# Windowed attention with 64x32 row tiles on TensorE, one head per half of the array, keys and values without zero blocks, and the feed-forward hidden layer in one PSUM bank

## The chip, the core and the metric

The kernel runs on one NeuronCore of a Trainium2 chip. A core has five engines that run side by side: TensorE (PE in the profile; its weight loads are shown as PEld), VectorE (DVE), ScalarE (ACT), GpSimd (POOL) and SyncE (SP), which here only issues DMAs. They are kept in step by semaphores. The metric is device time in microseconds for one execution; the kernel before takes 2605.0 us as the median of three runs (2604.25 to 2606.4).

## The reference

Eight sequences of 256 tokens and 128 channels pass through four stages, each wrapped in a layer norm before and after and a residual. Stage 1 is a linear attention, stage 2 is a stack of six layers of windowed attention plus gated feed-forward, stage 3 is a causal attention with a position bias, stage 4 is a mixture of eight experts. The change is in stage 2, whose layer is:

```
x = attn_layer(shift_tokens(x)) + x
x = ffn_layer(shift_tokens(x)) + x

attn_layer: q, k, v = split(x @ Wqkv)          # 16 heads of 64
            q, k = rotary(l2norm(q)), rotary(l2norm(k))
            window of 32 queries sees its own 32 keys and the 32 before
            sim = 8 * q @ k.T, masked; attn = softmax(sim); out = attn @ v
            return concat(out) @ Wo
ffn_layer:  a, gate = split(layernorm(x) @ W1 + b1)   # 341 wide each
            return (a * gelu(gate)) @ W2 + b2
```

All of it is in fp32.

## The kernel before

Stage 2 treats a (layer, sequence) pair as one item, so there are 6 x 8 = 48 items. The program is a software pipeline of steps t, each of eight slots s = 0 to 7, written out by hand in the same order on each engine (`step` at the end of each engine's part). In step t, item t is projected and rotated, item i = t - 1 goes through attention, and item f = t - 2 through the output projection and the feed-forward. The order of the code is the order of the work; every engine takes its instructions in that order and waits on semaphores.

The pieces, with the lines by which the profile names them:

- `projection` (PE L527): 512 columns of q or k for 128 tokens, one per slot, into bank 0 or 1. `squares` (ACT L900) and `parts` (DVE L1211) read it; `norms` (DVE L1218) follows at each odd slot, and POOL rotates and normalises (L1519 to L1527). `turn` (PE L538) transposes the rotated piece four slots later; `take_turned` (ACT L922 for queries, L925 and L926 for keys) copies it to `qT` or `kT`.
- `kT` holds for each pair of heads two blocks of 64 rows times keys: head 0 in rows 0 to 63 of the first, head 1 in rows 64 to 127 of the second, and zeros elsewhere. So one matmul with 128 rows and 32 columns of weights (the queries of one window, both heads) streams 2 x 64 columns and gives both heads' scores. `scores` (PE L563) does this for 4 pairs and 4 windows: 16 matmuls that write four 32-partition strips of bank 3. The bank has been seeded with the mask by `seed` (DVE L1235).
- `shift_scores` (DVE L1223, L1227) subtracts the row maximum, `exps` (ACT L933) takes the exponential, `turn_probs` (PE L572) transposes, `take_probs` (ACT L938) copies.
- `values` (PE L548) makes v; `take_values` (ACT L912) copies its two 64-row halves to `vp`, where each head has 64 columns and a one, with zeros in the other head's half of the rows; SP copies every second window's rows by DMA (`spread_values`). `weigh` (PE L584) is again 16 matmuls per group, 128 rows by 32 columns of weights, streaming 130 columns. `divide_out` (DVE L1241, L1245) divides by the sum, `turn_out` (PE L595, into bank 4) and `take_out` (ACT L945) give the transposed output.
- `project_out` (PE L604), a layer norm (L412, L418, POOL L1531, L425, DVE L1101 to L1110, L1258), `hidden` (PE L618) for three blocks c = 0, 1, 2 of the feed-forward, `gelu` (ACT L951), `gate` (DVE L1264), `contract` (PE L626) and two residual adds (DVE L1252, L1270). The three blocks of `hidden` use banks 2, 4 and 2, so block 1 shares a bank with `turn_out`.

Exp and Gelu need different ACT function tables, so ACT loads a table twice per item, before the first `gelu` and before the `exps` after the last.

Each fp32 matmul appears as two records in the trace (and its weight load as two), a transpose as one.

Of the kernel before, what the change touches and what calls it, by code (L numbers as in the profile page):

```python
# [33 lines left out]
VB = 2 * (DH + 1)  # L34
# [36 lines left out]
HD_BANK = (2, 4, 2)  # L71
# [9 lines left out]
def build(nc, a, out):  # L81
    ctx = ExitStack()
    with ctx:
# [6 lines left out]
        bank = [ctx.enter_context(nc.psum_tensor(f"bank{i}", [P, 512], F32)) for i in range(5)]  # L90
# [48 lines left out]
        kT = sb("kT", [P, PAIRS, 2, KW])  # L139
# [15 lines left out]
        kTf = kT[:, :, :, :].rearrange("p a b t -> p (a b t)")  # L155
# [21 lines left out]
        bias = kTf[:, 0:H * S].rearrange("p (h t) -> p h t", h=H)  # L177
# [15 lines left out]
        mw2 = vflat[:, NE * EF:2 * NE * EF].rearrange("p (e c n) -> p e c n", e=NE, c=4)  # L193
# [77 lines left out]
        def _(sp):  # L271
# [73 lines left out]
            def layer(l, first, last):  # L345
                for n in range(B):
                    t = l * B + n
                    sp.wait_ge(v_done, 8 * t + 2)
# [8 lines left out]
                    sp.wait_ge(v_done, 8 * t + 4)  # L357
# [12 lines left out]
                    sp.wait_ge(v_done, 8 * t + 6)  # L370
# [8 lines left out]
                    sp.wait_ge(v_done, 8 * t + 8)  # L379
# [16 lines left out]
            sp.dma_start(bias, bass.AP(relu_dram.ap().tensor, 0, [[1, P], [384, H], [1, S]])).then_inc(rel_in, 16)  # L396
# [11 lines left out]
        def _(pe):  # L408
# [132 lines left out]
            def values(i, w, odd):  # L541
# [4 lines left out]
                wait(pe, v_done, 8 * i + 2 * w)  # L546
# [6 lines left out]
            def scores(i, k):  # L553
# [21 lines left out]
            def weigh(i, k):  # L575
# [31 lines left out]
            def hidden(i, c):  # L607
# [4 lines left out]
                if c == 1:  # L612
                    wait(pe, ot_done, 4 * i + 4 + min(3, 4 * (ITEMS - 1 - i)))
                if c == 2:
                    pe.wait_ge(h_done, 3 * i + 1)
                n = P if c < 2 else FFR
                for half in range(2):
                    mm = nc.tensor.matmul(bank[HD_BANK[c]][0:n, half * S:half * S + S], w1[:, half * FF + c * P:half * FF + c * P + n],  # L618
# [53 lines left out]
            nc.tensor.matmul(bank[3][:, :], ident_bf, maskv[:, 0, :], start=True, stop=True).then_inc(seeded, 1)  # L672
# [176 lines left out]
        def _(act):  # L849
# [52 lines left out]
            def take_values(i, j):  # L902
# [803 lines left out]
```

## Time and profile before

| | value |
|---|---|
| median of 3 runs | 2605.0 us (2604.25 to 2606.4) |
| the profiled execution's own time | 2607.13 us |
| its span | 2605.3 us |
| stage 2 in full flow, as cut here | 250 to 1950 us |
| one step in full flow | 37.21 us |
| mean granted TensorE clock | 0.967, 1.00 in full flow |

Times in the profile are microseconds from the start of the span. The busy time of an engine is the union of its instructions; matmuls overlap in the array, so a record of 275 ns may advance the engine by much less. In full flow the steps repeat to within a hundredth of a microsecond, so the rows of one step stand for all. The step shown starts with the projection of slot 1 at 1052.68 and ends with that of the next step at 1089.89; its slots 2 to 7 start their projections at 1056.82, 1060.58, 1064.28, 1068.54, 1072.94 and 1078.20, and slot 0 of the next step at 1082.82.

### The profile page before, as it was taken

Reading aid. Unit: us, or ns where it says so; the run is one execution under the profiler, and the core shown is the slowest. Engines: PE = TensorE matmul, PEld = TensorE weight load, DVE = VectorE, ACT = ScalarE, POOL = GpSimd, SP = SyncE. Lnnn points to the kernel's source line nnn. Section 1 sums busy time; section 2 is a strip of 40 time slices with the busy share of each in tenths; the row PEclk is TensorE's granted clock in tenths of the full one; section 3 lists DMA queues with packets and bytes.
Section 4 is the critical chain, followed back from the end, with each engine's and each line's share of the span. In section 5 each row is a group of like instructions: output and inputs, shape, how many; then the busy total and the mean of one; then the engine's idle time right before and its main releaser. Section 6 shows DMA issues by size and latency. Waiting matters only on the chain.

```text
span 2605.3 us, 57541 instructions
## 1 busy us (share of the span) xinstructions
PE 2383.1 (91%) x22655; PEld 1632.9 (63%) x22655; DVE 1763.3 (68%) x2708; ACT 1625.6 (62%) x3162; POOL 1605.3 (62%) x931
## 2 busy tenths in 40 slices
PE   5769999999999999999999999999997888889998
PEld 3436666666666666666666666666665666656665
DVE  2348777777777777777777777777774888852332
ACT  1127777777777777777777777777773666643332
POOL 1039878887888788878887888788872222301111
PEclk8879999999999999999999999999997999989999
DMA  4002223222232222322233222322223000000000
GB/s 107 0 21 59 53 55 75 69 63 55 59 79 69 55 59 62 78 63 59 53 78 71 59 54 54 87 66 54 54 56 102 1 1 1 1 1 5 5 2 8
DMA packets 77196, 127.11 MB, mean 49 GB/s; under 512 B 24948, under 2 KB 48770, under 8 KB 76930
## 3 DMA queue, kind: packets, MB, share of 16 engines
q1 hardware_dynamic: 76930, 123.42, 20.3%
q8 instruction: 184, 3.01, 0.5%
q14 instruction: 82, 0.67, 0.1%
HBM read 26.56 MB, written 1.07 MB: 11 GB/s over the span
## 4 chain that ended last, share of the span: by engine, by line
PE 45%; DVE 26%; issue 13%; ACT 12%; POOL 4%; DMA 0%; SPq 0%; ACTq 0%; POOLq 0%; DVEq 0%
DVE qk L1211 7%; PE bank L604 7%; PE bank L527 5%; PE bank L563 5%; PE bank L813 4%; PE obank L584 4%; DVE n L1218 4%; PE bank L618 3%; ACT qk L900 3%; DVE bank L1235 3%; PE obank L823 2%; PE bank L823 2%; DVE sh L1227 2%; DVE mx L1223 2%; DVE mx L1365 2%
## 5 line engine op out<-in xcount | busy, mean ns | idle before, releaser
L1211 DVE TENSOR_TENSOR qk<-bank,tab 128x1024 f32<-128x1024 f32 x384 | 468.7, 1221 | 308.4 <-ACT qk L900 308.4
L1519 POOL TENSOR_TENSOR qk<-qk 128x1024 f32<-128x1024 f32 x192 | 454.6, 2368 | 284.0 <-DVE qk L1211 284.0
L1523 POOL TENSOR_TENSOR rn<-n2m,cst 128x16 f32<-128x16 f32 x192 | 562.6, 2930 | 16.0
L527 PE MATMUL bank<-wqk,xs 128*128 128x512 f32 x768 | 404.4, 609 | 46.0 <-ACT kT L926 43.0
L1527 POOL TENSOR_TENSOR qk<-qk,rn 128x1024 f32<-128x1024 f32 x192 | 365.2, 1902 | 28.2 <-POOL rn L1523 0.9
L900 ACT ACTIVATE qk<-bank 128x512 f32<-128x512 f32 x384 | 227.1, 591 | 213.8 <-PE bank L527 208.4
L538 PEld LDWEIGHTS bank<-cst,qk 128*128 128x128 f32 x1536 | 192.3, 141 | 210.5 <-issue 186.4
L1531 POOL TENSOR_TENSOR lnr<-lnv,cst 128x2 f32<-128x2 f32 (+1 forms) x88 | 66.3, 753 | 382.4 <-DVE lnv L1105 382.4
L538 PE MATMUL bank<-cst,qk 128*128 128x128 f32 x1536 | 231.7, 274 | 7.5 <-POOL qk L1527 7.5
L1218 DVE TENSOR_REDUCE n<-qk 128x16 f32<-128x1024 f32 x192 | 232.1, 1209 | 0.0
L912 ACT COPY vp<-lnbank 64x512 f32<-64x512 f32 x384 | 225.0, 586 | 9.4
L933 ACT ACTIVATE px<-sh 128x512 f32<-128x512 f32 x192 | 121.0, 630 | 153.9 <-DVE sh L1227 153.3
L563 PE MATMUL bank<-kT,qT 128*32 128x128 f32 x6144 | 208.0, 275 | 7.6 <-DVE bank L1235 1.3
L584 PE MATMUL obank<-vp,pT 128*32 128x130 f32 x6144 | 209.2, 274 | 0.0
L548 PE MATMUL lnbank<-wv,xs 128*64 128x512 f32 x768 | 208.0, 620 | 0.0
L563 PEld LDWEIGHTS bank<-kT,qT 128*32 128x32 f32 x6144 | 159.0, 109 | 50.8 <-issue 32.7
L527 PEld LDWEIGHTS bank<-wqk,xs 128*128 128x128 f32 x768 | 134.5, 191 | 78.1 <-ACT kT L926 54.6
L604 PE MATMUL bank<-aoT,wo 128*128 128x256 f32 x768 | 178.6, 385 | 0.7 <-DVE Z L1270 0.7
L595 PEld LDWEIGHTS bank<-cst,ao 128*128 128x128 f32 x768 | 80.3, 140 | 155.4 <-issue 153.4
L584 PEld LDWEIGHTS obank<-vp,pT 128*32 128x32 f32 x6144 | 177.3, 110 | 0.3 <-issue 0.3
L618 PE MATMUL bank<-lnt,w 128*128 128x256 f32 (+1 forms) x576 | 157.3, 397 | 2.7 <-DVE lnt L1258 1.7
L604 PEld LDWEIGHTS bank<-aoT,wo 128*128 128x128 f32 x768 | 142.0, 190 | 27.9 <-issue 10.5
(195 smaller groups left out, 4387.8 us busy)
## 6 DMA issues: line engine op xcount, KB each, us to landing
vp<-vp SPq DMA_DIRECT2D x672, 130.0 KB, 2.4
wqk<-in_L_ffn_Wqkv SPq DMA_DIRECT2D x24, 256.0 KB, 3.1
wv<-in_L_ffn_Wqkv SPq DMA_DIRECT2D x6, 512.0 KB, 3.6
wo<-in_L_ffn_Wo SPq DMA_DIRECT2D x6, 512.0 KB, 4.2
xs<-Z SPq DMA_DIRECT2D x48, 64.0 KB, 2.0
xs<-Z SPq DMA_DIRECT2D x48, 63.8 KB, 2.0
kT<-rel_by_distance SPq DMA_DIRECT2D x1, 2048.0 KB, 8.1
vp<-in_L_ffn_w SPq DMA_DIRECT2D x1, 2048.0 KB, 13.2
```

The lines of the kernel that those rows point to most:

```text
L527: nc.tensor.matmul(bank[s % 2][:, :], xs[:, odd, WIN + r * P:WIN + r * P + P], wqk[:, lo:lo + 512], start=True, stop=True).then_inc(p_full, 1)
L538: mm = nc.tensor.transpose(bank[(s + 1) % 2][:, q * P:q * P + P], rot[:, c, q * P:q * P + P], ident)
L563: mm = nc.tensor.matmul(s[WIN * w:WIN * w + WIN, q * P:q * P + P], qT[:, 4 * g + q, lo:lo + WIN], keys if w % 2 else keys[:, :, ::-1, :], ...
L584: mm = nc.tensor.matmul(obank[WIN * w:WIN * w + WIN, q // 2, (q % 2) * VB:(q % 2) * VB + VB], pT[:, k % 2, q * P + w * WIN:q * P + w * WIN ...
L604: mm = nc.tensor.matmul(bank[2][:, 0:S], wo[:, c, :], aoT[:, c, :], start=(c == 0), stop=(c == PAIRS - 1))
L618: mm = nc.tensor.matmul(bank[HD_BANK[c]][0:n, half * S:half * S + S], w1[:, half * FF + c * P:half * FF + c * P + n], lnt[:, S:2 * S], sta ...
L900: nc.scalar.activation(qk[:, square_of(s), :], bank[s % 2][:, :], ACT.Square).then_inc(sq_done, 1)
L1211: tt(qk[:, both, :].rearrange("p o (h d) -> p o h d", d=DH), heads(bank[c % 2][:, :]).unsqueeze(1).broadcast_to([P, 2, PAIRS, DH]), table. ...
L1218: red(n2[:, m % 2, :], qk[:, lo:lo + 2, :].rearrange("p a (h d) -> p (a h) d", d=DH), AX, ALU.add).then_inc(n2_raw, 1)
L1519: tt(direct, direct, swapped, ALU.add).then_inc(sum_done, 1)
L1523: tt(rn[:, m % 2, :], n2m[:, :], const("mhalf"), ALU.pow).then_inc(rn_done, 1)
L1527: tt(whole, whole, rn[:, m % 2, :].unsqueeze(2).broadcast_to([P, H, DH]), ALU.mult).then_inc(rot_done, 1)
```

## The change

`kT` has one block per pair, with head 0 in rows 0 to 63 and head 1 in rows 64 to 127, and no zeros; `vp` has 65 columns per pair instead of 130. A matmul of `scores` and of `weigh` now uses 64 rows and 32 columns, for one head. There are 32 per group instead of 16, each streaming 64 (65) columns instead of 128 (130). Head 0's results go to one PSUM bank and head 1's to the next: banks 3 and 4 (`sbank`) for scores, the two of `obank` for the weighing. Bank 4 is therefore no longer free for `turn_out`, which moves to the second bank of `obank`, nor for block 1 of `hidden`, which moves to bank 2. So each block of `hidden` now waits until `gate` has read the block before. The mask seed goes to half of two banks. ACT copies a group of keys, and a block of values, with one instruction instead of two. On ACT, `gelu` of block 0 moves from the start of slot 5 to behind `take_turned`; on DVE `gate` of block 0 moves behind `norms`. The scratch of stage 3 (the bias) and stage 4 (`w2` of the experts) that lived in the halved tensors has other places; `relu_dram` is read by two DMAs.

```diff
-VB = 2 * (DH + 1)
+VB = DH + 1
...
-        bank = [ctx.enter_context(nc.psum_tensor(f"bank{i}", [P, 512], F32)) for i in range(5)]
+        bank = [ctx.enter_context(nc.psum_tensor(f"bank{i}", [P, 512], F32)) for i in range(3)]
+        sbank = ctx.enter_context(nc.psum_tensor("sbank", [P, 2, 512], F32))
+        bank += [sbank[:, 0, :], sbank[:, 1, :]]
...
-        kT = sb("kT", [P, PAIRS, 2, KW])
+        kT = sb("kT", [P, PAIRS, KW])
...
-                s = bank[3]
                 for q in range(4):
                     for w in range(4):
                         lo = r * P + w * WIN
-                        keys = kT[:, 4 * g + q, :, lo:lo + 2 * WIN].rearrange("p o (s j) -> p o s j", s=2)
-                        mm = nc.tensor.matmul(s[WIN * w:WIN * w + WIN, q * P:q * P + P], qT[:, 4 * g + q, lo:lo + WIN],
-                                              keys if w % 2 else keys[:, :, ::-1, :], start=False, stop=True,
-                                              skip_group_check=True)
+                        for o in range(2):
+                            own = slice(64 * o, 64 * o + 64)
+                            keys = kT[own, 4 * g + q, lo:lo + 2 * WIN].rearrange("p (s j) -> p s j", s=2)
+                            mm = nc.tensor.matmul(sbank[WIN * w:WIN * w + WIN, o, q * DH:q * DH + DH],
+                                                  qT[own, 4 * g + q, lo:lo + WIN],
+                                                  keys if w % 2 else keys[:, ::-1, :], start=False, stop=True,
+                                                  skip_group_check=True)
...
                 wait(pe, ao_done, 4 * i + k)
+                wait(pe, ot_done, 4 * i + k)
                 for q in range(4):
                     for w in range(4):
-                        mm = nc.tensor.matmul(obank[WIN * w:WIN * w + WIN, q // 2, (q % 2) * VB:(q % 2) * VB + VB],
-                                              pT[:, k % 2, q * P + w * WIN:q * P + w * WIN + WIN],
-                                              vp[:, 4 * r + w, 4 * g + q, :], start=True, stop=True)
+                        for o in range(2):
+                            own = slice(64 * o, 64 * o + 64)
+                            mm = nc.tensor.matmul(obank[WIN * w:WIN * w + WIN, o, q * VB:q * VB + VB],
+                                                  pT[own, k % 2, q * P + w * WIN:q * P + w * WIN + WIN],
+                                                  vp[own, 4 * r + w, 4 * g + q, :], start=True, stop=True)
...
             def turn_out(i, k):
                 pe.wait_ge(ao_done, 4 * i + k + 1)
-                wait(pe, ot_done, 4 * i + k)
-                if k == 3 and i >= 1:
-                    pe.wait_ge(h_done, 3 * i - 1)
                 for q in range(4):
-                    mm = nc.tensor.transpose(bank[4][:, q * P:q * P + P], ao[:, k % 2, q * P:q * P + P], ident)
+                    mm = nc.tensor.transpose(obank[:, 1, q * P:q * P + P], ao[:, k % 2, q * P:q * P + P], ident)
...
-                if c == 1:
-                    wait(pe, ot_done, 4 * i + 4 + min(3, 4 * (ITEMS - 1 - i)))
-                if c == 2:
-                    pe.wait_ge(h_done, 3 * i + 1)
+                else:
+                    pe.wait_ge(h_done, 3 * i + c)
...
-                for o in (1, 0):
-                    lo = 64 * o
-                    src = vbank[lo:lo + 64, :].rearrange("p (a d) -> p a d", d=DH)
-                    cols = slice(o * (DH + 1), o * (DH + 1) + DH)
-                    nc.scalar.copy(vp[lo:lo + 64, 2 * j + 1, :, cols], src).then_inc(v_done, 1)
+                nc.scalar.copy(vp[:, 2 * j + 1, :, 0:DH], vbank[:, :].rearrange("p (a d) -> p a d", d=DH)).then_inc(v_done, 1)
...
-                    nc.scalar.copy(kT[0:64, pairs, 0, lo:lo + P], src[0:64])
-                    last = nc.scalar.copy(kT[64:P, pairs, 1, lo:lo + P], src[64:P])
+                    last = nc.scalar.copy(kT[:, pairs, lo:lo + P], src)
...
-                    if s in (5, 7) and p2:
-                        gelu(f, s - 5)
+                    if s == 7 and p2:
+                        gelu(f, 2)
...
-                    if s == 6 and p2:
-                        gelu(f, 1)
+                    if s in (5, 6) and p2:
+                        gelu(f, s - 5)
```

The first place is ACT in slots 5 and 6 of a step. Before, it read (L951 is `gelu`, L933 `exps`, L900 `squares`, L925 and L926 the keys' copies, L945 `take_out`, L938 `take_probs`):

```order
L933 ACTIVATE px<-sh 128x512 [waits pt_full,sh_done]
L951 ACT_TABLE_LOAD
L951 ACTIVATE ge<-bank,b1g 128x256 [waits hd_full]
L900 ACTIVATE qk<-bank 128x512 [waits n2_raw,p_full]
L925 COPY kT<-bank 64x4x128 [waits sc_full,t_full]
L926 COPY kT<-bank 64x4x128
L945 COPY aoT<-bank 128x4x128 [waits ot_full]
L938 COPY pT<-obank 128x512 [waits o_full,pt_full]
L900 ACTIVATE qk<-bank 128x512 [waits n2_raw,p_full]
```

Now it reads (L952 is `gelu`, L906 `squares`, L927 the keys' copy):

```order
L934 ACTIVATE px<-sh 128x512 [waits pt_full,sh_done]
L906 ACTIVATE qk<-bank 128x512 [waits n2_raw,p_full]
L927 COPY kT<-bank 128x4x128 [waits sc_full,t_full]
L952 ACT_TABLE_LOAD
L952 ACTIVATE ge<-bank,b1g 128x256 [waits hd_full]
L946 COPY aoT<-obank 128x4x128 [waits ot_full]
L939 COPY pT<-obank 128x512 [waits o_full,pt_full]
L906 ACTIVATE qk<-bank 128x512 [waits n2_raw,p_full]
```

The table load and the first `gelu` have moved behind the squares of slot 5 and the keys' copy, and that copy is one instruction.

The second place is PE from slot 6 to the projection of slot 7. Before, it read (L618 is `hidden`, blocks 1 and 2, L563 `scores`, L584 `weigh`):

```order
L538 MATMUL bank<-cst,qk 128x128 x3
L618 MATMUL bank<-lnt,w 128x256 [waits ot_done]
L618 MATMUL bank<-lnt,w 128x256
L563 MATMUL bank<-kT,qT 32x128 [waits seeded,t_done]
L563 MATMUL bank<-kT,qT 32x128 x15
L584 MATMUL obank<-vp,pT 32x130 [waits ao_done,pt_done]
L584 MATMUL obank<-vp,pT 32x130 x15
L618 MATMUL bank<-lnt,w 85x256 [waits h_done]
L618 MATMUL bank<-lnt,w 85x256
L527 MATMUL bank<-wqk,xs 128x512 [waits t_done]
```

Now it reads (L623 is `hidden`, L569 `scores`, L594 `weigh`):

```order
L543 MATMUL bank<-cst,qk 128x128 x3
L623 MATMUL bank<-lnt,w 128x256 [waits h_done]
L623 MATMUL bank<-lnt,w 128x256
L569 MATMUL sbank<-kT,qT 32x64 [waits seeded,t_done]
L569 MATMUL sbank<-kT,qT 32x64 x31
L594 MATMUL obank<-vp,pT 32x65 [waits ot_done,ao_done,pt_done]
L594 MATMUL obank<-vp,pT 32x65 x31
L623 MATMUL bank<-lnt,w 85x256 [waits h_done]
L623 MATMUL bank<-lnt,w 85x256
L532 MATMUL bank<-wqk,xs 128x512 [waits t_done]
```

The sequence is the same; there are twice as many small matmuls of half the width, and the first `hidden` row waits for `gate` of block 0 instead of for a copy out of bank 4.

## Rows read from the trace of the kernel before

**Rows 1.** The page: span, and busy time of each engine with its share.
```profile
span 2605.3 us, 57541 instructions
PE 2383.1 (91%) x22655; PEld 1632.9 (63%) x22655; DVE 1763.3 (68%) x2708; ACT 1625.6 (62%) x3162; POOL 1605.3 (62%) x931
```

**Rows 2.** Windows: length, busy time and records per engine, granted clock, DMA share, GB/s.
```profile
250.00:1950.00 1700.00, 1645.11 (x17964) 1124.43 (x17966) 1291.56 (x1868) 1239.66 (x2192) 1382.43 (x775) 1.00 0.27 63
1052.68:1089.89 37.21, 36.04 (x396) 24.63 (x394) 28.36 (x41) 27.14 (x48) 30.31 (x18) 1.00 0.30 69
```

**Rows 3.** Waits of PE from 250 to 1950: total us, times, longest.
```profile
PE bank L527 <- ACT kT L926: 42.0, 46, 0.9
```

**Rows 4.** Groups by line: shapes, count, busy us, mean ns, idle before.
```profile
L912 ACT COPY vp<-lnbank 64x512 f32<-64x512 f32 x384 | 225.0, 586 | 9.4
L926 ACT COPY kT<-bank 64x512 f32<-64x512 f32 x192 | 111.6, 581 | 2.2
L922 ACT COPY qT<-bank 128x512 f32<-128x512 f32 x192 | 111.4, 580 | 8.3 <-PE bank L538 8.3
L1218 DVE TENSOR_REDUCE n<-qk 128x16 f32<-128x1024 f32 x192 | 232.1, 1209 | 0.0
L1245 DVE TENSOR_TENSOR ao<-obank,rd 128x512 f32<-128x512 f32 x192 | 132.8, 692 | 6.6
```

**Rows 5.** Windows of L563 alone: length, PE and PEld busy with records begun or in flight.
```profile
1038.15:1038.18 0.03, 0.03 (x4) 0.03 (x5) 1.00 0.00 0
1038.37:1038.48 0.11, 0.11 (x12) 0.11 (x8) 1.00 0.00 0
```

**Rows 6.** Timeline of PE, slots 3 to 0: start, us, engine, line, operation, count.
```profile
1064.01 0.43 PE L425 MATMUL bank<-cst,lnr 128*128 128x128 f32 x2
1064.28 1.02 PE L527 MATMUL bank<-wqk,xs 128*128 128x512 f32 x2
...
1068.54 1.02 PE L527 MATMUL bank<-wqk,xs 128*128 128x512 f32 x2
...
1072.94 1.13 PE L527 MATMUL bank<-wqk,xs 128*128 128x512 f32 x2 [0.91 <-ACT kT L926]
...
1074.34 1.03 PE L618 MATMUL bank<-lnt,w 128*128 128x256 f32 x4
...
1077.27 1.09 PE L618 MATMUL bank<-lnt,w 128*85 128x256 f32 x4
1078.20 1.02 PE L527 MATMUL bank<-wqk,xs 128*128 128x512 f32 x2
...
1084.43 1.08 PE L563 MATMUL bank<-kT,qT 128*32 128x128 f32 x32
1085.30 1.10 PE L584 MATMUL obank<-vp,pT 128*32 128x130 f32 x32
1086.33 3.72 PE L604 MATMUL bank<-aoT,wo 128*128 128x256 f32 x16
```

**Rows 7.** Timeline of POOL, the layer norm's power in slot 3, and its last rotation.
```profile
1063.26 0.70 POOL L1531 TENSOR_TENSOR lnr<-lnv,cst 128x2 f32<-128x2 f32 x1
...
1088.38 1.90 POOL L1527 TENSOR_TENSOR qk<-qk,rn 128x1024 f32<-128x1024 f32 x1
```

**Rows 8.** Timeline of ACT and DVE, slots 2 to 6.
```profile
1061.19 0.63 ACT L933 ACTIVATE px<-sh 128x512 f32<-128x512 f32 x1 [0.92 <-DVE sh L1227]
1061.73 0.59 ACT L900 ACTIVATE qk<-bank 128x512 f32<-128x512 f32 x1
...
1068.94 0.63 ACT L933 ACTIVATE px<-sh 128x512 f32<-128x512 f32 x1 [1.30 <-DVE sh L1227]
1069.58 1.28 ACT L951 ACT_TABLE_LOAD   x1
1070.88 0.47 ACT L951 ACTIVATE ge<-bank,b1g 128x256 f32<-128x256 f32 x1
1071.25 0.59 ACT L900 ACTIVATE qk<-bank 128x512 f32<-128x512 f32 x1
...
1075.13 1.22 DVE L1211 TENSOR_TENSOR qk<-bank,tab 128x1024 f32<-128x1024 f32 x1
```

More of the change, by code:

```diff
@@ L70 @@
 LAG = 4
-HD_BANK = (2, 4, 2)
 GATE_OPS, TAIL_OPS = 13, 6
@@ L175, in build @@
         bout = sb("bout", [P, 1])
-        bias = kTf[:, 0:H * S].rearrange("p (h t) -> p h t", h=H)
+        tabf = tab[:, :, :, :, :].rearrange("p l k r d -> p (l k r d)")
+        bias = [f[:, 0:PAIRS * S].rearrange("p (h t) -> p h t", h=PAIRS) for f in (kTf, tabf)]
         relv = sb("relv", [WIN, H])
@@ L395, in _ @@
             sp.wait_ge(o_full, 4 * ITEMS)
-            sp.dma_start(bias, bass.AP(relu_dram.ap().tensor, 0, [[1, P], [384, H], [1, S]])).then_inc(rel_in, 16)
+            sp.wait_ge(parts_done, 8 * ITEMS)
+            for half in range(2):
+                sp.dma_start(bias[half], bass.AP(relu_dram.ap().tensor, half * PAIRS * 384, [[1, P], [384, PAIRS], [1, S]]))\
+                    .then_inc(rel_in, 16)
             sp.dma_start(mw1, a["L1_ffn_w1"].rearrange("e m f -> m e f")).then_inc(ld_s4, 16)
@@ L544, in values @@
                     pe.wait_ge(ld_v, (i // B) * 16 + 16)
-                wait(pe, v_done, 8 * i + 2 * w)
+                wait(pe, v_done, 4 * i + w)
                 for o in range(2):
@@ L611, in hidden @@
                     pe.wait_ge(ld_w1, (i // B) * 16 + 16)
-                if c == 1:
-                    wait(pe, ot_done, 4 * i + 4 + min(3, 4 * (ITEMS - 1 - i)))
-                if c == 2:
-                    pe.wait_ge(h_done, 3 * i + 1)
+                else:
+                    pe.wait_ge(h_done, 3 * i + c)
                 n = P if c < 2 else FFR
                 for half in range(2):
-                    mm = nc.tensor.matmul(bank[HD_BANK[c]][0:n, half * S:half * S + S], w1[:, half * FF + c * P:half * FF + c * P + n],
+                    mm = nc.tensor.matmul(bank[2][0:n, half * S:half * S + S], w1[:, half * FF + c * P:half * FF + c * P + n],
                                           lnt[:, S:2 * S], start=True, stop=True)
@@ L670, in _ @@
             pe.wait_ge(masks_cast, 1)
-            nc.tensor.matmul(bank[3][:, :], ident_bf, maskv[:, 0, :], start=True, stop=True).then_inc(seeded, 1)
+            nc.tensor.matmul(bank[3][:, :], ident_bf, maskv[:, 0, :], start=True, stop=True)
+            nc.tensor.matmul(bank[4][:, :], ident_bf, maskv[:, 0, :], start=True, stop=True).then_inc(seeded, 1)
             step(0, 0, True, False, False, False)
@@ L945, in take_out @@
                 nc.scalar.copy(aoT[:, 4 * g:4 * g + 4, r * P:r * P + P],
-                               bank[4][:, :].rearrange("p (a n) -> p a n", a=4)).then_inc(ot_done, 1)
+                               obank[:, 1, :].rearrange("p (a n) -> p a n", a=4)).then_inc(ot_done, 1)
             def gelu(i, c):
@@ L950, in gelu @@
                 act.wait_ge(hd_full, 3 * i + c + 1)
-                nc.scalar.activation(ge[0:n, c, :], bank[HD_BANK[c]][0:n, S:2 * S], ACT.Gelu,
+                nc.scalar.activation(ge[0:n, c, :], bank[2][0:n, S:2 * S], ACT.Gelu,
                                      bias=b1g[0:n, c, bass.ds(i // B, 1)]).then_inc(ge_done, 1)
@@ L1218, in norms, with by_pair @@
                 red(n2[:, m % 2, :], qk[:, lo:lo + 2, :].rearrange("p a (h d) -> p (a h) d", d=DH), AX, ALU.add).then_inc(n2_raw, 1)
+            def by_pair(ap):
+                return ap.rearrange("p (q o n) -> p o q n", o=2, n=DH)
             def shift_scores(i, k):
-                b = 3
                 dve.wait_ge(sc_full, 4 * i + k + 1)
-                red(mx[:, k % 2, :], heads(bank[b][:, :]), AX, ALU.max).then_inc(mx_done, 1)
+                sc = sbank[:, :, 0:4 * DH].rearrange("p o (q n) -> p o q n", n=DH)
+                m = mx[:, k % 2, :].rearrange("p (o q) -> p o q", o=2)
+                red(m, sc, AX, ALU.max).then_inc(mx_done, 1)
                 dve.wait_ge(mx_done, 4 * i + k + 1)
                 wait(dve, px_done, 4 * i + k - 1)
-                tt(heads(sh[:, k % 2, :]), heads(bank[b][:, :]), mx[:, k % 2, :].unsqueeze(2).broadcast_to([P, PAIRS, DH]),
-                   ALU.subtract).then_inc(sh_done, 1)
+                tt(by_pair(sh[:, k % 2, :]), sc, m.unsqueeze(3).broadcast_to([P, 2, 4, DH]), ALU.subtract).then_inc(sh_done, 1)
             def seed(i, k):
@@ L1234, in seed @@
                     dve.wait_ge(sh_done, n)
-                    nc.vector.tensor_copy(bank[3][:, :], maskv[:, (n % 4) // 2, :]).then_inc(seeded, 1)
+                    nc.vector.tensor_copy(sbank[:, :, 0:4 * DH], maskv[:, (n % 4) // 2, :].rearrange("p (o n) -> p o n", o=2))\
+                        .then_inc(seeded, 1)
             def divide_out(i, k):
@@ L1263, in gate @@
                 dve.wait_ge(ge_done, 3 * i + c + 1)
-                nc.vector.scalar_tensor_tensor(out=hT[0:n, c, :], in0=bank[HD_BANK[c]][0:n, 0:S], scalar=b1a[0:n, c, l],
+                nc.vector.scalar_tensor_tensor(out=hT[0:n, c, :], in0=bank[2][0:n, 0:S], scalar=b1a[0:n, c, l],
                                                in1=ge[0:n, c, :], op0=ALU.add, op1=ALU.mult).then_inc(h_done, 1)
@@ L1289, in step @@
                         parts(t, s)
-                    if s in (5, 6) and p2:
-                        gate(f, s - 5)
+                    if s == 6 and p2:
+                        gate(f, 1)
                     if s in (0, 2, 4) and p1:
@@ L1297, in step @@
                         norms(t, s // 2)
+                    if s == 5 and p2:
+                        gate(f, 0)
                     if s in (1, 3, 5) and p1:
@@ L1361, in attend @@
                 part = sh[:, m % 2, :].rearrange("p (h n) -> p h n", n=w)
-                tt(part, bank[3 + m % 2][:, :].rearrange("p (h n) -> p h n", n=w), bias[:, hs[0]:hs[-1] + 1, S - w:S]
-                   if r == 0 else bias[:, hs[0]:hs[-1] + 1, :], ALU.add).then_inc(s3["add"], 1)
+                lo = hs[0] % PAIRS
+                tt(part, bank[3 + m % 2][:, :].rearrange("p (h n) -> p h n", n=w), bias[hs[0] // PAIRS][:, lo:lo + len(hs), S - w:S],
+                   ALU.add).then_inc(s3["add"], 1)
                 dve.wait_ge(s3["add"], NJ * b + m + 1)
@@ L1386, in step3 @@
                         finish(b - 1, m, u + 2 if next_batch else u)
-            dve.wait_ge(rel_in, 16)
+            dve.wait_ge(rel_in, 32)
             for slot in range(9):
```

25 lines of the change are left out of this document (12 added, 13 removed).

## The prediction, made before the changed kernel was run

> **What bounds the kernel now.** I read the page first: PE is busy for 91% of the span, no other engine for over 68% [rows 1]. Then the windows: in full flow, 1700 us of the span, PE is busy 1645 us at a granted clock of 1.00. One step there is 37.21 us, with PE busy 36.04, POOL 30.31, DVE 28.36, ACT 27.14 [rows 2]. So PE bounds a step. Then the waits: the only wait of PE worth a line is 46 times 0.9 us, for the second key copy on ACT [rows 3]. Last the timeline of one step, for which hand-over would end last once PE is faster [rows 6 to 8]. There are 46 steps (t = 2 to 47) with all parts on, so a saving per step counts 46 times. All sums stand against the profiled execution's own 2607.1 us; the median of the runs is 2.1 us below it.
>
> **The small matmuls.** A group of scores takes 1085.30 - 1084.43 = 0.87 us for its 32 records, one per 27 ns; a weighing takes 1086.33 - 1085.30 = 1.03 us, of which the next, full-width matmul's start is some 0.16 [rows 6]. Each record is in flight for about 275 ns, so some ten overlap: the four column strips work side by side. What sets 27 ns? In the steady part a window of 0.11 us, a hundred-odd ns for 128 columns on each of four strips, holds 12 records begun or in flight [rows 5]. The transposes of the same 128 columns on the whole array also advance by about that. So each strip is busy streaming its own 128 columns, and 0.87 us is four strips times 8 rounds of 109 ns. It is not issue: at the start of a group four matmuls with their weight loads begin within 0.03 us, 7 ns a pair [rows 5].
>
> After the change there are 64 records per group of half the width on 8 tiles, so again 8 rounds, of 54 ns each: 0.44 us. At 7 ns a pair, 64 pairs also need 0.45. That is the lower end. The trace has no matmul on half the rows, and nowhere a pair rate under 27 ns that lasts longer than a few instructions. The upper end is the present lasting rate: 64 x 27.2 = 1.74 us. The row tiles not overlapping at all gives 0.87. I take 0.44, since the row nearest in kind (four different tiles begun within 0.03 us) speaks for it, and keep 0.44 to 1.74 for the range.
>
> Two rules of the Trainium skill bear on this, and pull apart. The row first: four starts in 0.03 us on different strips. "TensorE: Matmul & The Clock Gate", part "Measured speedup vs the span model", gives some 4 ns per further tile, and by that the group is bound by streaming, 0.44 us. The same page, in "Wait — 56ns, not 53.3ns?", says that start-to-start never drops below about 25 ns however small the matmul. If that held across tiles a group would be 64 x 25 = 1.6 us, and this change would lose. The trace contradicts it for the first four, and can't say for sixty-four.
>
> **What of it is on the path.** 8 groups x 0.43 = 3.4 us per step looks like the saving, but most of it falls where PE would only wait earlier.
> - Slot 1 to slot 4's projection. Before the projection of 1064.28 PE runs the layer norm's L425 at 1064.01, which needs POOL's power of 1063.26 + 0.70 = 1063.96 [rows 6, 7]. POOL got there by a chain that starts with slot 1's parts and is not shortened. The two groups of slot 2 buy nothing.
> - Slot 4. The two groups bring slot 5's projection forward by 0.85, to 1067.69, but `parts` of slot 5 doesn't wait for it: ACT squares only after `exps` at 1068.94 [rows 8]. Again nothing.
>
> **The moved table load and merged copies.** In slot 5, ACT now squares right behind `exps`. By slot 2's rows squares start 0.54 after exps [rows 8]: 1069.48 instead of 1071.25. So table load and Gelu no longer hold up `parts`, the key copy and PE. Behind the squares (0.48) and one key copy of 0.58 instead of two (a 128-row copy costs no more than a 64-row one, 580 and 581 ns [rows 4]), the table load starts at 1070.54 and Gelu at 1071.84, ending 1072.31. PE has the copy at 1070.55 and its own work until 1071.05, so slot 6's projection starts at 1071.05 instead of 1072.94, and the transposes end at 1072.35.
>
> New wait 1: block 1 of `hidden` needs `gate` of block 0. DVE: parts of slot 5 at 1070.10, norms 1.12 [rows 4], so gate at 1072.36 to 1072.82. `hidden` starts at 1072.85 instead of 1074.34 after waiting 0.5. Queued behind it on PE are scores (two groups, now 1.0 together) and block 2.
> New wait 2: block 2 needs `gate` of block 1. ACT: take_out and take_probs end at 1073.2, squares to 1073.68, query copy to 1074.26, Gelu to 1074.73. DVE: parts of slot 6 at 1073.82 instead of 1075.13 [rows 8], ends 1074.96, gate to 1075.42. So block 2 starts at 1075.45 instead of 1077.27 [rows 6]: 1.82 earlier, though PE stands for 0.75. Queued behind is slot 7's projection.
>
> From there to the scores of slot 0 (1078.20 to 1084.43 [rows 6]) the order is as before and the chain goes through the second table load, exps, squares, parts, norms and seed, none of them changed: everything shifts by 1.82. Then scores, weighing and L604 follow each other on PE with nothing between, and the two groups save 0.43 each. L604 ends 1.82 + 0.86 = 2.68 earlier. POOL's last rotation, 1088.38 + 1.90 [rows 7], shifts with slot 7 to 1088.5, early enough for slot 2 of the next step.
>
> **At nothing.** The DVE operations keep their element counts; one that reads two banks already takes 692 ns [rows 4]. The merged value copies take 4 x 0.59 off ACT, which is not the bound; what hides it is ACT's own idle time. The extra wait of `weigh` for `take_out`, done 2 us before, costs nothing. SP's copies of values move half the bytes and nobody waits for them. Stage 3 and 4 keep their work. The first and last steps give perhaps 2 us together.
>
> **Sum.** 46 x 2.68 = 123, + 2 = 125 at most. Each new wait adds a hand-over that I can only place to about 0.05 us, so I take off 46 x 0.05 = 2. 2607.1 - 123 = 2484, against the median 2482. I forecast 2483 us; its own range is 2455 to 2525, from groups of 0.44 to 0.65 and hand-overs 0.5 us off in a step.
>
> **Rivals.**
> 1. *Row tiles don't overlap.* Tiles above each other share the strip's output and take turns: a group stays 0.87. For it: the trace shows only strips side by side. Against: each head has its own bank. Then only the ACT part is left, and PE is the bound again: slot 6's projection at 1071.89, hidden 1073.19, scores and weighing 1.90, block 2 at 1075.97 instead of 1077.27, 1.30 per step. 2607.1 - 46 x 1.30 = 2547, as median 2545.
> 2. *Issue or weight loading becomes PE's bound, slower.* In PE's eight small groups per step, 64 weight loads and 64 matmuls must be fed; if the lasting rate is the 27 ns of today, a group is 1.74. PE is then the bound everywhere, and each group's 0.87 extra counts 8 times, less the 1.30 of rival 1: + 5.7 per step, 2607.1 + 46 x 5.7 = 2869. It decides from 0.87 + 1.30 / 8 = 1.03 us per group, or 16 ns a pair: above that the kernel is slower than before. For it: every sustained stretch shows 27. Against: that is exactly the streaming time, and bursts show 7.
> By the page's 25 ns floor, as an estimate, the group is 1.6 us and the time about 2820.
> 3. *One bank for hidden.* The waits for `gate` are longer than placed, as ACT's queue is full there: each of the two 1 us longer gives 2.68 - 2.0 = 0.68 per step, 2576.
>
> **Chances.** Forecast 0.60, rival 1 0.15, rival 2 0.18, rival 3 0.05, else 0.02. Faster (by over 0.2%, about what a measurement can tell here): 0.60 + 0.15 + most of rival 3 = 0.78. Within 0.2%: 0.03, a group near 1.03 us. Slower: 0.19. The range 2455 to 2600 holds the forecast, rivals 1 and 3, and leaves out rival 2 and little else.
>
> **What would show it.** In the profile after: scores L569 to weighing L594 0.44 apart and 64 records (0.87: rival 1; over 1.03: rival 2). The wait of PE for the key copy gone; in its place PE waits of about 0.5 and 0.75 us per step at L623 for DVE's gate. A step of about 34.5 us with PE busy below 33. The layer norm's matmul of slot 3 (L430 in the changed file) waiting for POOL by about 0.8 us per step. ACT's copies at 192 per line, 580 ns. If the step is 34.5 but groups are 0.87, the walk is wrong though the time is right.

## The result, and the profile after

The changed kernel takes 2697.85 us (median of 4 runs, 2693.34 to 2700.99) against 2605.07 us of the kernel before on the same chip: 1.0354 times the time, interval 1.034 to 1.0367. It is slower, where I forecast 2483 us and a range to 2600. The prediction was wrong in its sign.

The page after, against [rows 1] (its columns as there), with its line on instruction fetches: packets, MB, share of the DMA engines.

```profile
span 2692.8 us, 81640 instructions
PE 2362.3 (88%) x34944; PEld 1606.0 (60%) x34944; DVE 1765.9 (66%) x2707; ACT 1366.7 (51%) x2778; POOL 1601.7 (59%) x931
q8 instruction: 279, 4.57, 0.7%
```

The same line of the kernel before:

```profile
q8 instruction: 184, 3.01, 0.5%
```

PE's share fell from 91 to 88% although the span grew: PE stands idle more. PE has 12,289 more matmul records and as many more weight loads. 4.57 MB in 279 packets is 16.4 KB each; the kernel before fetched 184 such packets. The 95 more packets carry 24,578 more instructions, 259 to a packet. So one packet is about 256 of PE's instructions, or 128 pairs of weight load and matmul.

The window in full flow, with the columns of [rows 2], and then PE's waits in it (total us, times, longest), which answer to [rows 3].

```profile
250.00:1950.00 1700.00, 1547.75 (x28221) 1046.28 (x28206) 1237.98 (x1782) 945.88 (x1740) 1316.89 (x738) 0.97 0.15 37
```

```profile
PE obank L594 <- issue: 107.3, 56, 2.5
PE bank L430 <- POOL lnr L1538: 18.6, 27, 0.7
PE bank L611 <- issue: 9.9, 5, 2.2
PE bank L532 <- issue: 6.4, 5, 1.7
```

The wait for the key copy is gone, as forecast. In its place PE is idle at "issue" (127.8 us with two smaller rows, 3.3 at L423 and 0.9 at L543), in the middle of work for which the profile shows no wait, most of it in `weigh` (L594). There is none at L623 for `gate`. The step, 37.21 us before, is now irregular, 35.9 to 43.2 from one slot 0 to the next, on average 39.1 (37.21 plus the 87.5 us of longer span over 46 steps).

The timeline of PE has both cases within 10 us; the columns are those of [rows 6].

```profile
1076.00 1.13 PE L623 MATMUL bank<-lnt,w 128*128 128x256 f32 x4
1077.06 0.86 PE L569 MATMUL sbank<-kT,qT 64*32 64x64 f32 x64
1077.72 0.85 PE L594 MATMUL obank<-vp,pT 64*32 64x65 f32 x64
1078.59 1.09 PE L623 MATMUL bank<-lnt,w 128*85 128x256 f32 x4
...
1085.01 0.60 PE L543 MATMUL bank<-cst,qk 128*128 128x128 f32 x4
1085.75 0.85 PE L569 MATMUL sbank<-kT,qT 64*32 64x64 f32 x64
1086.51 0.64 PE L594 MATMUL obank<-vp,pT 64*32 64x65 f32 x38
1089.02 0.66 PE L594 MATMUL obank<-vp,pT 64*32 64x65 f32 x26 [1.88 <-issue]
```

At 1077.06 the scores take 0.66 us until the weighing starts, and the weighing 0.87 until the next matmul: before it was 0.87 and 1.03 [rows 6]. So the tiles do overlap. At 1086.51 the same weighing breaks off after 38 records and goes on 1.88 us later. In the trace's DMA records a packet of instructions began at 1086.73. All 69 stops at "issue" from 250 to 1950 look so: each ends 2.2 to 3.0 us, in the median 2.46, after an instruction packet began. And if one counts PE's records from the start (matmuls, weight loads and the semaphore instructions between them), all 69 stops lie a whole multiple of 256 apart, to within one. So they all fall where one packet ends and the next begins.

What follows such a stop stands in windows of the same step (length, busy time of PE and PEld, then the other engines; the clock is third from the end).

```profile
1085.00:1086.50 1.50, 1.36 (x69) 1.10 (x68) 1.50 (x4) 1.29 (x3) 1.50 (x2) 1.00 0.00 0
1086.50:1089.00 2.50, 0.64 (x47) 0.48 (x39) 1.91 (x3) 0.80 (x2) 2.42 (x2) 1.00 0.23 57
1089.00:1091.00 2.00, 1.98 (x29) 1.59 (x29) 0.90 (x2) 0.10 (x1) 1.86 (x2) 0.51 0.32 78
1091.00:1093.00 2.00, 2.00 (x7) 1.62 (x6) 0.00 (x0) 0.00 (x0) 0.60 (x1) 0.63 0.00 0
1093.00:1095.00 2.00, 2.00 (x11) 1.55 (x10) 0.23 (x1) 0.00 (x0) 0.00 (x0) 1.00 0.00 0
```

After 1.88 us without work the granted clock is about 0.5 (1.2 GHz) for some 3.5 us of the output projection. In the second window the clock still shows 1.00: the loss comes behind the stop. Not every stop has it: in the clock's records from 250 to 1950, 32 of the 69 are followed by half clock, 116 us in all. The kernel before has none there.

The line groups that answer to [rows 4]:

```profile
L1250 DVE TENSOR_TENSOR ao<-obank,rd 128x512 f32<-128x512 f32 x192 | 132.8, 692 | 6.8 <-DVE rd L1246 0.2
L927 ACT COPY kT<-bank 128x512 f32<-128x512 f32 x192 | 111.2, 579 | 8.4 <-PE bank L543 8.3
```

ACT's and DVE's parts came as costed: one copy for two, at 579 ns (607 for the values), and DVE's reading of two banks still at 692 ns.

### The profile page after: what moved, and what is told of

Read it like the earlier page. It is cut to its first block, busy times and chain, and to the rows that moved or that the text cites. A ratio compares the mean times of both kernels' runs of the same rounds, so it can differ in the third digit from the quotient of the medians.

```text
span 2692.8 us, 81640 instructions
## 1 busy us (share of the span) xinstructions
PE 2362.3 (88%) x34944; PEld 1606.0 (60%) x34944; DVE 1765.9 (66%) x2707; ACT 1366.7 (51%) x2778; POOL 1601.7 (59%) x931
## 3 DMA queue, kind: packets, MB, share of 16 engines
q8 instruction: 279, 4.57, 0.7%
HBM read 26.56 MB, written 1.07 MB: 10 GB/s over the span
## 4 chain that ended last, share of the span: by engine, by line
PE 61%; DVE 13%; POOL 10%; issue 10%; ACT 5%; SPq 0%; DMA 0%; POOLq 0%; ACTq 0%; DVEq 0%
PE bank L532 8%; PE bank L611 7%; PE bank L623 6%; PE obank L594 5%; PE sbank L569 5%; PE bank L543 4%; PE lnbank L553 4%; POOL rn L1530 3%; DVE qk L1211 3%; POOL qk L1526 3%; PE bank L819 2%; POOL qk L1534 2%; PE obank L829 2%; PE sbank L829 2%; PE obank L602 2%
## 5 line engine op out<-in xcount | busy, mean ns | idle before, releaser
L532 PE MATMUL bank<-wqk,xs 128*128 128x512 f32 x768 | 419.3, 629 | 9.4 <-issue 6.4
L906 ACT ACTIVATE qk<-bank 128x512 f32<-128x512 f32 x384 | 227.9, 593 | 378.5 <-PE bank L532 378.0
L543 PEld LDWEIGHTS bank<-cst,qk 128*128 128x128 f32 x1536 | 198.7, 145 | 225.2 <-issue 211.1
L594 PE MATMUL obank<-vp,pT 64*32 64x65 f32 x12288 | 179.0, 226 | 115.8 <-issue 115.8
L543 PE MATMUL bank<-cst,qk 128*128 128x128 f32 x1536 | 238.2, 279 | 8.0 <-POOL qk L1534 6.0
L594 PEld LDWEIGHTS obank<-vp,pT 64*32 64x32 f32 x12288 | 142.7, 105 | 129.1 <-issue 123.8
L611 PE MATMUL bank<-aoT,wo 128*128 128x256 f32 x768 | 195.7, 411 | 11.7 <-issue 11.0
L611 PEld LDWEIGHTS bank<-aoT,wo 128*128 128x128 f32 x768 | 154.0, 206 | 41.9 <-issue 16.0
L623 PE MATMUL bank<-lnt,w 128*128 128x256 f32 (+1 forms) x576 | 171.6, 424 | 5.4 <-DVE hT L1268 3.5
L602 PEld LDWEIGHTS obank<-cst,ao 128*128 128x128 f32 x768 | 81.0, 141 | 157.4 <-issue 122.5
L569 PE MATMUL sbank<-kT,qT 64*32 64x64 f32 x12288 | 164.9, 224 | 7.6 <-DVE sbank L1238 1.4
L569 PEld LDWEIGHTS sbank<-kT,qT 64*32 64x32 f32 x12288 | 134.8, 105 | 49.4 <-issue 47.5
L1030 ACT ACTIVATE px<-sh,mx 128x128 f32<-128x128 f32 (+1 forms) x256 | 113.7, 445 | 52.5 <-DVE mx L1372 51.0
```

Of the source, the lines that this page charges most:

```text
L532: nc.tensor.matmul(bank[s % 2][:, :], xs[:, odd, WIN + r * P:WIN + r * P + P], wqk[:, lo:lo + 512], start=True, stop=True).then_inc(p_full, 1)
L543: mm = nc.tensor.transpose(bank[(s + 1) % 2][:, q * P:q * P + P], rot[:, c, q * P:q * P + P], ident)
L569: mm = nc.tensor.matmul(sbank[WIN * w:WIN * w + WIN, o, q * DH:q * DH + DH], qT[own, 4 * g + q, lo:lo + WIN], keys if w % 2 else keys[:, : ...
L594: mm = nc.tensor.matmul(obank[WIN * w:WIN * w + WIN, o, q * VB:q * VB + VB], pT[own, k % 2, q * P + w * WIN:q * P + w * WIN + WIN], vp[own ...
L611: mm = nc.tensor.matmul(bank[2][:, 0:S], wo[:, c, :], aoT[:, c, :], start=(c == 0), stop=(c == PAIRS - 1))
L623: mm = nc.tensor.matmul(bank[2][0:n, half * S:half * S + S], w1[:, half * FF + c * P:half * FF + c * P + n], lnt[:, S:2 * S], start=True, ...
```

## The experiments

Theory 1: PE's instructions come in packets of 256, each fetched only when PE enters the last one it holds, and scores and weighing back to back (2 x 128 instructions in about 1.5 us) outrun that. (When exactly a packet is fetched turned out to be less simple; that stands under `bursts`.) Theory 2: the stop belongs to the row tiles or their banks, whatever stands around them. All ratios are to the kernel before on the same chip.

### `spaced`: the row-tiled groups moved apart

```
+ if s in (2, 4) and p1: weigh(i, s // 2)     # before projection(t, s, odd)
...
- if s % 2 == 0 and p1: weigh(i, s // 2)      # behind scores
+ if s == 6 and p2: hidden(f, 2)
+ if s == 0 and p2: project_out(f)
+ if s in (0, 6) and p1: weigh(i, s // 2)
```

> The changed kernel with PE's two small-matmul groups of a slot pulled apart: in slots 2 and 4 the weighing goes ahead of the projection and the scores stay behind the transposes; in slot 6 block 2 of hidden stands between them, in slot 0 the output projection. Nothing else is moved and no instruction is added. Theory 1 (instruction supply): PE's instructions arrive in pieces of 16 KB, 256 instructions, each about 2.4 us after its request, and some 110 are left when it is requested; scores and weighing together are 256 matmul and weight-load records in 1.5 us and outrun that, a single group of 128 does so only when the request falls just ahead of it. It expects PE's idle time inside L594 to fall from 105 us to under 30, the granted clock in full flow to go back from 0.97 to about 1.00, and 2480 to 2540 us. Theory 2 (the row tiles themselves): the weighing's bank, its wait for take_out or the 64-row form stops PE. It expects about as many stops as before inside the weighing, and 2650 us or more.

Measured: 2616.69 us, ratio 1.004 (1.0026 to 1.0054). Its window and PE's waits:

```profile
250.00:1950.00 1700.00, 1621.86 (x29684) 1057.29 (x29690) 1293.40 (x1867) 994.60 (x1827) 1382.87 (x774) 1.00 0.15 39
PE bank L623 <- DVE hT L1272: 39.3, 75, 0.7
PE obank L594 <- ACT pT L943: 27.6, 91, 0.5
PE sbank L569 <- issue: 7.2, 18, 0.6
```

With the same tiles, banks and instruction count the idle time at "issue" falls from 127.8 us to some 10 (2.5 of it in `weigh`), the clock is 1.00 again, and 81 us come back. Theory 2 falls. My figure for the time, 2480 to 2540, was 77 us too low: the weighing ahead of the projection waits for ACT's copy of the probabilities, twice a step (27.6 us), and `hidden` waits for `gate`, also twice a step (39.3 us). These are waits of this order and of the single bank, not of the tiles.

### `split`: apart, but nothing ahead of the projection

```
+ if s == 0 and p2: project_out(f)            # all between scores and weigh
+ if s == 2 and p2: ln_var_pe(S, LN_S2 + f, bank[2])
+ if s in (4, 6) and p2: hidden(f, s - 4)
```

> The changed kernel with something wide put between the scores and the weighing of each even slot, and nothing put ahead of a projection: the output projection in slot 0, the layer norm's variance in slot 2, hidden block 0 in slot 4, block 2 in slot 6. Supply theory, as the first runs left it: a new piece of 256 instructions is asked for when PE enters the last one it holds and is usable some 3.5 us later, so PE stops where it runs 256 instructions in less. The pair now takes 0.65 + gap + 0.65 us, with gaps 3.6, 0.5, 1.0 and 0.9: no stops in slot 0, rarer and shorter ones (at most 1.2 to 1.7 us) in the others; idle time inside the groups under 50 us, granted clock 0.99 to 1.00 in full flow, 2510 to 2560 us. If the stops have nothing to do with supply but with weighing directly behind scores, none is left: under 2500.

Measured: 2583.93 us, ratio 0.9918 (0.9895 to 0.9942). PE's waits:

```profile
PE bank L623 <- DVE hT L1268: 30.8, 48, 1.1
PE obank L594 <- issue: 19.8, 24, 1.4
PE bank L430 <- POOL lnr L1538: 19.1, 39, 1.0
```

The wait on ACT's probabilities is gone; the one for `gate` in the single bank stays (0.64 us, about once a step) and now has the weighing queued behind it. Of the 24 stops that remain in the weighing, 18 are in slot 4, 4 in slot 6 and 2 in slot 2, where one block of `hidden` or the layer norm's matmuls is all that lies between; slot 0, with the output projection between, has none. All parts of the change are in here, in another order, and it is faster than before, not slower: the 114 us between it and the changed kernel are the order's. The time was above my range by 24 us.

### `scores_only` and `weigh_only`: one group on row tiles, the other as before

```
# scores_only: row-tiled scores, and
- for o in range(2): ... pT[own, ...], vp[own, ...]
+ mm = nc.tensor.matmul(obank[...], pT[:, ...], vp[:, ...], start=True, stop=True)
# weigh_only: row-tiled weighing, and
- for o in range(2): ... qT[own, ...], keys (kT[own, ...])
+ mm = nc.tensor.matmul(bank[3][...], qT[:, ...], keys, start=False, ...)
```

> The changed kernel with the weighing put back to 128x32 tiles with zero blocks in vp (16 matmuls of 130 columns, two value copies on ACT); scores stay on 64x32 tiles, the order of work stays. A pair of groups is then 128 + 64 = 192 records. Theory 1 (instruction supply): stops of about 2 us still occur, at under half the count of the changed kernel, most in or at the end of the scores or in the weighing; 2540 to 2620 us. Theory 2 (row-tiled weighing is what stops): no stops, a step of about 35.2 us, 2505 to 2530 us.

> The changed kernel with the scores put back to 128x32 tiles with zero blocks in kT (16 matmuls of 128 columns into one bank, two key copies on ACT); the weighing keeps 64x32 tiles, the order of work stays. The mirror image of scores_only. Supply theory: 64 + 128 = 192 records in a pair, no 256 in less than 3.5 us, so hardly any stop although the weighing is row-tiled: granted clock 0.99 or more, 2545 to 2575 us. If row-tiled weighing itself is what stops PE, the stops stay (50 or more, 100 us and more) and the time is above 2640.

Measured: `scores_only` 2551.36 us, ratio 0.9788 (0.9773 to 0.9802), the fastest kernel of this study and faster than both given ones. `weigh_only` 2586.48, ratio 0.9926 (0.9898 to 0.9954). `scores_only`, fetches, window and waits:

```profile
q8 instruction: 231, 3.78, 0.6%
250.00:1950.00 1700.00, 1652.63 (x24124) 1116.09 (x24123) 1310.96 (x1906) 1127.18 (x2031) 1392.32 (x788) 0.99 0.29 67
PE bank L430 <- POOL lnr L1541: 16.0, 45, 1.0
PE obank L592 <- issue: 3.5, 6, 1.6
```

`weigh_only`, waits:

```profile
PE obank L591 <- issue: 16.3, 14, 1.6
PE bank L620 <- DVE hT L1264: 14.3, 48, 1.0
```

A pair of groups is now 192 instructions instead of 256, and either kind alone runs: neither row tiles in `sbank` nor in `obank` are the fault. The fetched packets (231) lie midway between 184 and 279, with the instruction count. PE waits for POOL's layer norm 45 times for 0.36 us: the wait that the prediction had put at 0.8. `scores_only` lies in the range of theory 1, but its stops are fewer and shorter than the 2 us that it gave. `weigh_only` is 11 us above its range. Some stops remain, more of them with row-tiled weighing: 6 of its steps take 39.0 to 40.0 us, most of the rest 36.22. I had expected hardly any, since no 256 instructions there run in under 3.5 us. That much is so: up to each of the 14 stops of the weighing PE took 7.3 to 9.2 us for its last 256 instructions. It stopped all the same; what that says of the theory stands under `bursts`. Why the weighing is worse than the scores at the same count isn't settled; the instructions that stand ahead of each group differ, and I made no run for it.

### `order_only` and `scores_old_order`: Gelu and gate moved alone, and not moved

```
- if s in (5, 7) and p2: gelu(f, s - 5)       # order_only, in before; ahead of parts
+ if s == 7 and p2: gelu(f, 2)
+ if s in (5, 6) and p2: gelu(f, s - 5)       # behind the key copy; gate(f, 0) likewise
# scores_old_order: scores_only with these lines turned back
```

> The kernel before with one thing alone: gelu of block 0 behind take_turned on ACT and gate of block 0 behind norms on DVE. By the walk of the prediction with two key copies of 0.58 instead of one, block 2 of hidden starts 1.07 us earlier per step (76.20 instead of 77.27), so 46 x 1.07 = 49 us less, 2556 us; both theories expect that, and no stops of PE in the small groups. If the walk is wrong it shows here: same as before would mean that the ACT order was not what held PE.

> scores_only (row-tiled scores, 128x32 weighing) with gelu and gate of block 0 back in their places of the kernel before, so that the table load again stands between exps and squares in slot 5. What is left of the change is the narrower scores, the one key copy and hidden in one bank. Order_only gave 0.72 us per step for the new order by itself. If the two parts add, this kernel is 0.6 to 1.0 us per step slower than scores_only: 2580 to 2597 us; if the new order is worth nothing once scores are shorter, 2551.

Measured: `order_only` 2571.35 us, ratio 0.9864 (0.985 to 0.9879), a step of 36.49, 0.72 less than before, where I had expected 1.07. `scores_old_order` 2612.16, ratio 1.0021 (1.0003 to 1.0039), most steps 37.0 and on average 37.27, against 37.22 before: parts that simply add would have given 2580 to 2597. PE's waits in `scores_old_order`:

```profile
PE sbank L569 <- DVE sbank L1241: 26.9, 48, 1.0
PE bank L532 <- ACT kT L929: 16.2, 40, 0.4
```

and in `order_only`:

```profile
PE bank L618 <- ACT aoT L945: 12.1, 47, 1.0
```

The parts do not add. With ACT's old order, shorter scores and a single key copy only turn into waits: PE comes earlier and stands at the seed of the bank (0.56 us a time) and at the key copy (0.40). With the new order the same edits give (2571.35 - 2551.36) / 46 = 0.43 us a step (36.49 - 35.72 = 0.77 in a step without stops), and the new order is worth (2612.16 - 2551.36) / 46 = 1.3 us a step instead of (2606.91 - 2571.35) / 46 = 0.77.

### `bursts` and `bursts_rest`: PE alone

PE's program without any wait once its tile is loaded (one run each, 539.16 and 493.07 us): long stretches of 128x32 and of 64x32 matmuls, then bursts with full-width matmuls between them.

```
for n in range(1280):
    nc.tensor.matmul(pb[n % 2][strip(n // 2), 0:64], w[own(n), 0:32], w[own(n), 0:64], ...)
...
for k in range(24):                       # bursts_rest, with r = 4, 3, 2, 1
    for n in range(64): ... as above
    for n in range(r): nc.tensor.matmul(wide[:, :], w[:, 0:P], w[:, :], ...)
```

> None of the reference's work is done (the output is zeros): PE alone, fed from one tile in SBUF, runs 640 matmuls of 128x32 weights and 128 columns back to back, then 1280 of 64x32 weights and 64 columns (the same streaming work at twice the instructions), then 16 bursts each of 16, 32 and 64 row-tiled matmuls (64, 128, 256 records) with seven 512-column matmuls between. Theory 1: the first stretch runs at 27 ns a pair (256 instructions in 3.5 us, longer than a fetch), the second is held by fetches at about 2.4 us per 256 instructions, near 19 ns a pair, not 7 to 8; bursts of 64 records never stop, bursts of 128 rarely, bursts of 256 in more than half of the cases, for about 2 us. Theory 2: the second stretch and all bursts behave alike, either 7 to 8 ns a pair throughout or stops at any length.

> None of the reference's work is done (the output is zeros). PE alone runs 24 bursts of 64 row-tiled matmuls (256 records) with 4, then 3, then 2, then 1 matmul of 512 columns (0.87 us, 4 records) between them. A burst takes 1.27 us, so a round takes 4.9, 4.1, 3.2 and 2.3 us if nothing stops. Supply theory: 256 instructions per about 3.5 us at most, so the first two stretches run without a stop and the last two settle at 3.6 to 3.9 us a round whatever the work in it, with stops of 0.4 to 0.7 and 1.3 to 1.6 us per round. A rival by which PE's queue simply needs a pause after a burst would show no difference between 4 and 1.

`bursts`, timeline of PE:

```profile
22.89 36.21 PE L116 MATMUL pb<-w 128*32 128x128 f32 x1280
...
76.39 2.85 PE L120 MATMUL pb<-w 64*32 64x64 f32 x271
81.17 1.47 PE L120 MATMUL pb<-w 64*32 64x64 f32 x128 [1.92 <-issue]
84.89 2.04 PE L120 MATMUL pb<-w 64*32 64x64 f32 x128 [2.26 <-issue]
88.35 2.04 PE L120 MATMUL pb<-w 64*32 64x64 f32 x128 [1.42 <-issue]
```

and its clock in two windows, the two kinds of matmul:

```profile
23.50:58.50 35.00, 34.80 (x1255) 33.92 (x1247) 0.00 (x0) 0.00 (x0) 1.00 0.02 5
77.00:144.00 67.00, 37.47 (x2492) 33.57 (x2477) 0.00 (x0) 0.00 (x0) 0.54 0.02 5
```

This is the clearest view of the cause. After what was already held, PE runs exactly 128 records (256 instructions with their weight loads), stops, and runs the next 128, one packet every 3.45 to 4 us. No other engine works and no other data moves meanwhile, so no other DMA, bank or engine is to blame. Half-sized matmuls take 26.7 ns each (68.3 us for 2560 records), where I had expected near 19; 128x32 ones of twice the work take 28.3 ns: tiling by rows gains nothing here that lasts. In the same kernel a burst of 128 records followed by 6 us of wide work never stopped. My expectation that over half of these would stop was a miss: without waits, what counts is the time that 256 instructions take.

`bursts_rest` puts a figure on that time, and turns down a pause that would follow every burst. Timeline of PE, with three, two and one wide matmul between bursts:

```profile
161.95 1.48 PE L124 MATMUL pb<-w 64*32 64x64 f32 x128
163.36 2.84 PE L126 MATMUL wide<-w 128*128 128x512 f32 x6
166.13 1.48 PE L124 MATMUL pb<-w 64*32 64x64 f32 x128
...
326.74 1.98 PE L133 MATMUL wide<-w 128*128 128x512 f32 x4
328.65 1.19 PE L131 MATMUL pb<-w 64*32 64x64 f32 x99
330.12 0.45 PE L131 MATMUL pb<-w 64*32 64x64 f32 x29 [0.28 <-issue]
...
455.32 1.28 PE L138 MATMUL pb<-w 64*32 64x64 f32 x105
457.39 0.42 PE L138 MATMUL pb<-w 64*32 64x64 f32 x23 [0.78 <-issue]
457.75 1.12 PE L140 MATMUL wide<-w 128*128 128x512 f32 x2
458.80 1.23 PE L138 MATMUL pb<-w 64*32 64x64 f32 x103
```

At 4.18 us of work per round (268 instructions) there is no stop. At 3.33 us (264) small ones come, mostly 0.2 to 0.3 us where I expected 0.4 to 0.7. With 2.47 us of work (260) nearly each round stops, and 20 rounds from 392.96 to 469.79 take 3.84 us each, within the 3.6 to 3.9 expected. So, without waits, the limit lies at about 3.5 us per 256 instructions (3.45 to 4.0 from one packet to the next), 13.6 ns an instruction or 27 ns a pair.

That limit alone does not give the stops of the changed kernel. Up to 43 of its 69 stops (83 of the 127.8 us) PE had taken 3.8 to 9.6 us for its last 256 instructions, more than the limit. At the stops of the two `bursts` kernels the next packet's DMA had begun 0.85 to 1.65 us after PE entered the packet before. In these 43 cases it begins over 2 us after, but always 0.96 to 1.59 us after the record of PE's wait ahead of the scores (L562). In 29 of the 43 no other DMA packet had begun in the 4 us before, so other traffic isn't the reason. The packet was asked for late, just as some 200 short instructions were let go. The stop above is one of them: PE entered the packet at 1080.96, the wait is recorded at 1085.64, the DMA began at 1086.73, PE stopped at 1087.14. That fits a fetch that goes by how far PE's instructions have been let past their waits, and not by the moment at which PE enters a packet. It is a reading of the trace: no run was made for it, and the moment of the request itself is in no record.

## Why the prediction was wrong

The step that failed is in "The small matmuls": "It is not issue: at the start of a group four matmuls with their weight loads begin within 0.03 us, 7 ns a pair". Four starts show how fast PE begins instructions that it holds. They don't show how fast new ones arrive, and that was the price I left out: the sum has no term for the fetch of instructions, neither in the groups nor under "At nothing". The runs put it at 127.8 us of stops and 116 us at half clock behind them in 1700 us of full flow. The kernel before sat just at both limits: its 27.2 ns a pair is the streaming of 128 columns on four strips, as I said, and also the 27 ns at which packets arrive. The change halves the first and doubles the number of instructions that the second is paid for.

Point by point:
- *(What bounds the kernel.)* Right, PE; but part of PE's bound was about to be its instructions, and the line on the instruction queue in the page (184 packets) was not used.
- *(A group, 0.44 us.)* The direction was right and rival 1 is refuted. First to last start is 0.64 us in the group at 1077.06, its first 32 pairs 8 ns apart and the last 32 12 ns, and the next matmul follows 0.66 and 0.87 us after the group's start. Over the full flow the medians are 0.76 and 0.78, against 0.90 and 1.00 before: of the 0.43 hoped for, some 0.14 and 0.22 are there.
- *(Only slot 0's groups on the path.)* Probably too strict. In `scores_only` a group of scores takes 0.79 us instead of 0.87 to 0.90, some 0.1 less, and it saves 0.43 us a step over `order_only` (0.77 without stops), as if all four groups of scores counted, less a POOL wait of 0.36 rather than 0.8. But `scores_only` also has the single key copy and `hidden` in one bank, so the share of the scores is argued and not shown.
- *(The moved table load, 1.82 us a step.)* Right in kind and too large: 0.72 to 0.77 alone, where 1.07 was expected, and 1.3 once the scores are shorter. The waits for `gate` that I placed at 0.5 and 0.75 appear where there are few stops (0.64 in `split`, 0.52 in `spaced`) and are hidden by the stops in the changed kernel.
- *(At nothing.)* Right: merged copies and DVE's reads cost what the rows said.
- *(Sum.)* In the changed kernel's own terms, a step of 39.1 us has 2.9 of stops (127.8 us over 43.5 steps) and, as an estimate, up to 1.3 of half clock: 116 us at half clock are 58 us of lost work. What is left, 34.9, is work and ordinary waits. Against the 34.5 forecast that is 46 x 0.4 = 18 us for the mis-sized groups and the order, 133 for the stops and up to 60 for the clock. 2484 + 18 + 133 + 60 = 2695, the profiled execution's 2694.8. As the 34.9 is a remainder, that this sum closes is no check of it.
- *(Rival 2, chance 0.18.)* Right in name and sign, wrong in shape. I priced it as 1.74 us for every group and 2869 us. But a group without a stop is short, and one with the end of a packet in it loses some 2 us at a time. Its deciding point of "1.03 us per group" has no meaning then: that depends on what stands around the group. It should have had more of the chance, since every lasting stretch of the trace showed 27 ns and only bursts of four showed less.

The Trainium skill's "TensorE: Matmul & The Clock Gate", in "Wait — 56ns, not 53.3ns?", would have put a floor of about 25 ns on each start. Across different tiles no such floor is there: in `bursts` the 128 pairs from 81.17 on start within 1.25 us, some 10 ns apart. That the lasting rate comes near 25 ns all the same (26.7) is due to the supply.

## What to carry to other kernels

Where PE takes less than 3.5 us for 256 of its instructions, weight loads counted, smaller tiles cannot pay for long: count instructions per stretch before cutting in two, and put long matmuls between groups of short ones. Staying above that limit is not enough: 43 of the 69 stops came above it, each with some 200 short instructions right behind a wait. So look at the instruction packets in the DMA records, too. A rate read from a few starts in a row is a rate of issue, not of supply; look for a stretch longer than 256 instructions. And a wait-free order comes first: the same edits of the scores and the key copy were worth nothing with ACT's old order and 0.43 us a step with the new one.

## What the runs showed of the hardware

- PE's instructions arrive in packets of 16.4 KB, 256 instructions each. `bursts` shows one per 3.45 to 4 us at the most, also with no other traffic; in the changed kernel a stop ends about 2.46 us after its packet's DMA began, and all 69 stops lie a multiple of 256 instructions apart, to within one.
- A stop of some 2 us is often, not always, followed by half clock: 32 of the 69 stops of the changed kernel are (0.51 and 0.63 in the windows after 1089), and their length does not tell which (1.74 to 2.43 us with it, 0.63 to 2.46 without). In `bursts`, with a stop of 1.4 to 2.3 us in each round of 3.45 to 4, the clock is 0.54. In the last stretch of `bursts_rest`, with stops of mostly 0.7 to 1.4 us in each round, PE is busy for 57.17 of 80 us and the granted clock is 1.00. Where between them the clock gives way wasn't measured.
- Matmuls of 64 rows by 32 columns on eight tiles do run side by side, into two banks, at some 10 ns a pair while instructions last (64 pairs in 0.64 us, 128 in 1.25 us).
